# A gated recurrence with a feed-forward block: the first block's states aligned and its y formed ahead of a check's result, late gates and three other steps in another order

## The chip, the cores and the metric

The kernel runs on one core of a Trainium2 chip. The metric is device time in microseconds (us) of one execution. Its engines have queues of their own and meet through semaphores only: TensorE (PE, matmul), VectorE (DVE), ScalarE (ACT), GpSimd (POOL), SyncE (SP, which issues DMAs).

## The reference

```python
def layer(x, W_in, b_in, W_gate, b_gate, A, Bm, C, D, W_out, b_out):
    u = x @ W_in + b_in
    g = sigmoid(x @ W_gate + b_gate)
    def step(h_prev, (u_t, g_t, x_t)):
        h_t = tanh(h_prev @ A + u_t @ Bm)
        y_t = h_t @ C.T + u_t @ D.T
        return h_t, g_t * y_t + (1 - g_t) * x_t
    return scan(step) @ W_out + b_out + x
def ffn(x, w1, b1, w2, b2):      # w1, w2 binarized: row mean of |w| times sign(w)
    return gelu(x @ bw1.T + b1) @ bw2.T + b2
x = layernorm(x + layer(x))
x = layernorm(x + ffn(x))
```

x has 2 sequences of 4096 rows of 256, the state 64, the hidden layer 1024 values. All is float32.

## The kernel before

The recurrence is sequential. The kernel cuts each sequence in 64 chunks of 64 steps and runs the 128 chunks side by side, one per column. It first runs the last 40 steps of every chunk from zero to guess the state with which the next one starts, and then all 64 steps from the guess (`sweep1`). `hu` holds for each step the state (partitions 0 to 63) and u (64 to 127); the state that belongs to a step is in the next slot. Steps go in blocks of four (16 blocks, `NB`), each a tile of 128 x 512 for either half of the 256 values.

**The check.** After the last step VectorE compares the end states with the guesses (lines 1246 to 1251: difference, largest, flag per row), TensorE counts the flags (918), VectorE casts the count to an integer (1253), and VectorE, ScalarE and TensorE each load it and branch. If the guesses were off by more than 2^-18 a repair runs the recurrence again 64 times. It isn't needed with these inputs, so all three jump over it. After it VectorE writes two small copies (1262, 1263); the first lets GpSimd go on, which sits still until then.

**The passage.** What follows ties the recurrence to the feed-forward blocks. By step, and with the line that the profile names:

- gates: TensorE multiplies x by W_gate (828 with operands split in a high and a low part, for blocks up to 11; 814 for 12 to 15), ScalarE applies the sigmoid (522). A gate is done in halves, one per 128 outputs, in banks 0 and 1. `GATED` is 11: blocks 11 to 15 are left for the passage.
- `align(n)` (1408): four VectorE copies move the states of block n one slot down, each after the one before, so that state and u of a step stand in one slot. Blocks 0 and 1 only.
- `whole_y_products(n)` (936): y from the aligned slots, in banks 2 and 3. From block 2 on `y_products` (947) takes split operands instead: `hu_high` on ScalarE (580) and `hu_low` on GpSimd (376).
- `less_x`, `gate_y` (VectorE, 1268 and 1274), `mix` (GpSimd, 384): gate times (y - x), plus x. `ys_high` (ScalarE, 560) and `ys_low` (GpSimd, 388) split it.
- `out_products` (TensorE, 965): times W_out, for a pair of row tiles. `add_bias` (GpSimd, 394) adds half of b_out to the reloaded x.
- `first_sum` (VectorE, 1280; it waits for both), spread and moments (1286, 1292), `first_rstd` (GpSimd, 410 and 412), `first_norm` (VectorE, 1302).
- for blocks 0 and 1 `x1_transposes` (TensorE, 974), then `x1_hi` (ScalarE, 569) and `x1_lo` (VectorE, 1314). `residual` (GpSimd, 404) adds b2.
- the feed-forward block in eight chunks c: `hidden` (TensorE, 991), gelu and `hidden_hi` (ScalarE, 585, 593), `hidden_lo` (VectorE, 1319), `ffn_out` (TensorE, 1003). hidden(c) waits for the low part of chunk c - 3.

The order on every engine is written out by hand in the program, and each does its list strictly in that order. From block 1 on `iteration(n)` gives each engine the same list for every block.

Of the kernel before, what the change touches and what calls it, by code (L numbers as in the profile page):

```python
# [39 lines left out]
P = 128  # L40
# [10 lines left out]
def gated_rnn_ffn(nc, x, W_in, b_in, W_gate, b_gate, A, Bm, C, D, W_out, b_out, w1, b1, w2, b2, out):  # L51
# [21 lines left out]
    with ExitStack() as ctx:  # L73
# [3 lines left out]
        def sem(name):  # L77
            return ctx.enter_context(nc.semaphore(name))
# [100 lines left out]
        s_shift = sem("states_aligned")  # L179
        s_huhi = sem("hu_hi_ready")  # L180
# [156 lines left out]
        def _(pool):  # L337
# [48 lines left out]
            def ys_low(b, m):  # L386
                pool.wait_ge(s_yhi, b * KD + m + 1)
                pool.tensor_tensor(ys_lo[:, m, :], gT[:, b, m, :], ys_hi[:, m, :].bitcast(F32),  # L388
                                   ALU.subtract).then_inc(s_ylo, 1)

            def add_bias(b):

                pool.wait_ge(s_xl, b * 16 + 16)
                pool.tensor_tensor(x_load[:, :, :], x_load[:, :, :],  # L394
                                   half_b_out[:, None, :].broadcast_to([P, STEPS, DM]), ALU.add).then_inc(s_xb, 1)
# [11 lines left out]
            def first_rstd(b, pair):  # L407
                tiles = slice(2 * pair, 2 * pair + 2)
                pool.wait_ge(s_v1, b * 2 + pair + 1)
                pool.tensor_tensor(rstd1[:, tiles], moments[:, 0, tiles, 1], eps[:, tiles], ALU.add).then_inc(s_e1, 1)  # L410
                pool.wait_ge(s_e1, b * 2 + pair + 1)
                pool.tensor_tensor(rstd1[:, tiles], rstd1[:, tiles], neg_half[:, tiles], ALU.pow).then_inc(s_rs1, 1)
# [41 lines left out]
            add_bias(0)  # L454
# [3 lines left out]
            ys_low(0, 1)  # L458
            first_rstd(0, 0)
# [41 lines left out]
        def _(act):  # L501
# [18 lines left out]
            def gate(j, m):  # L520
                act.wait_ge(s_gmm, j * KD + m + 1)
                nc.scalar.activation(gT[:, j, m, :], bank[m][:, :], ACT.Sigmoid,
                                     bias=b_gate_col[:, m:m + 1]).then_inc(s_g, 1)
# [129 lines left out]
            gate(GATED, 1)  # L653
            gate(GATED + 1, 0)
            ys_high(0, 0)
            gate(GATED + 1, 1)
            ys_high(0, 1)
# [7 lines left out]
            x1_hi(0, 1)  # L665
            ys_high(1, 1)
            gate(GATED + 3, 1)
            gate(GATED + 4, 0)
            gate(GATED + 4, 1)
# [13 lines left out]
            hidden_gelu(0, 5)  # L683
            x1_hi(1, 0)
            hidden_hi(0, 5)
# [34 lines left out]
        def _(pe):  # L720
# [197 lines left out]
            nc.tensor.matmul(bank[6][0:1, 0:1], gap_flag, ones[0:NS, 0:1], start=True, stop=True).then_inc(s_cnt, 1)  # L918
            gate_half(GATED, 1, gate_parts, 1)
# [11 lines left out]
            def whole_y_products(n):  # L931
                pe.wait_ge(s_shift, n * STEPS + STEPS)
                for m in range(KD):
                    if n > 0:
                        pe.wait_ge(s_t, n * KD - KD + m + 1)
                    nc.tensor.matmul(bank[2 + m][:, :], cd_t[:, m * P:(m + 1) * P],
                                     hu[:, bass.ds(n * STEPS, STEPS), :].rearrange("p s r -> p (s r)"),
                                     start=True, stop=True).then_inc(s_ymm, 1)
# [103 lines left out]
            pe.wait_ge(s_wsplit, 2)  # L1042

            whole_y_products(0)
            gate_half(GATED + 1, 1, gate_product)
            gate_half(GATED + 2, 0, gate_product)
            gate_half(GATED + 2, 1, gate_product)
            for pair in range(2):
                out_products(0, pair)
            whole_y_products(1)  # L1050
            gate_half(GATED + 3, 0, gate_product)
            for pair in range(2):
                x1_transposes(0, pair)
            gate_half(GATED + 3, 1, gate_product)
            gate_half(GATED + 4, 0, gate_product)
            gate_half(GATED + 4, 1, gate_product)
# [3 lines left out]

            hidden(0, 0)
            hidden(0, 1)
            out_products(1, 0)
# [10 lines left out]
            ffn_out(0, 3)  # L1074
            x1_transposes(1, 0)
            hidden(0, 6)
            x1_transposes(1, 1)
            y_products(3, 0)
            hidden(0, 7)
            ffn_out(0, 4)  # L1080
# [25 lines left out]
        def _(dve):  # L1106
# [138 lines left out]

            dve.wait_ge(s_h, 1 + WARM + L)
# [4 lines left out]
            nc.vector.tensor_scalar(gap_flag, gap_max, GUESS_TOLERANCE, None, ALU.is_gt).then_inc(s_cmp, 1)  # L1251
            dve.wait_ge(s_cnt, 1)
# [3 lines left out]
            with dve.If(differ):  # L1256
                nc.vector.tensor_copy(guess, end_state).then_inc(s_rh, 1)
                with dve.Fori(1, CHUNKS) as r:
                    dve.wait_ge(s_rh, r * (L + 1))
                    nc.vector.tensor_copy(guess, end_state).then_inc(s_rh, 1)  # L1260
                dve.wait_ge(s_rh, CHUNKS * (L + 1))
            nc.vector.tensor_copy(small[:, 31:32], inv_scale).then_inc(s_done, 1)
# [140 lines left out]
            def align(n):  # L1403

                for step in range(n * STEPS, (n + 1) * STEPS):
                    if step > 0:
                        dve.wait_ge(s_shift, step)
                    nc.vector.tensor_copy(hu[0:NS, step, :], hu[0:NS, step + 1, :]).then_inc(s_shift, 1)


            align(0)
# [37 lines left out]
            hidden_lo(0, 4)  # L1449
            x1_lo(1, 0)  # L1450
            hidden_lo(0, 5)
# [70 lines left out]
```

## Time and profile before

Median of 3 runs 459.25 us (457.73 to 459.54). The profiled execution took 457.62 us, its span (first to last instruction) is 455.8 us at a mean granted TensorE clock of 0.989.

| engine | busy us | share of the span | instructions |
|---|---|---|---|
| TensorE, matmul | 430.1 | 94% | 2719 |
| TensorE, weight load | 307.0 | 67% | 2719 |
| VectorE | 372.6 | 82% | 800 |
| ScalarE | 313.0 | 69% | 578 |
| GpSimd | 271.0 | 59% | 289 |

The recurrence ends near 119.7 us, the last gate is done near 148.9 us, and the rhythm of the feed-forward blocks begins near 172 us. The end of a matmul is modelled, so that the next may start a little ahead of it. In a timeline's row the idle time of the engine ahead of the row and the instruction that ended it stand in brackets.

### The profile page before, as it was taken

The page shows a single profiled execution, that of the slowest core. Times are in us where ns is not written, and L with a number is a line of the kernel's source. Part 1 is how long each engine was busy: PE and PEld are TensorE (multiplying, and loading weights), DVE is VectorE, ACT ScalarE, POOL GpSimd, SP SyncE. Part 2 cuts the span into 40 slices and gives each one's busy share as a digit, 9 for nine tenths or more (in the row PEclk, how much of TensorE's full clock was granted, in tenths as well). Part 3 has the DMA queues.
Part 4 walks back from the last instruction along what each step waited for, and adds up shares of the span by engine and source line. Part 5 has one row for each costly group of instructions (what it writes and reads, how often), then busy time and mean ns, then how long its engine had stood idle before and what let it go on. Part 6 is the DMA issues. An engine that isn't in the chain of part 4 may idle for free.

```text
span 455.8 us, 8144 instructions
## 1 busy us (share of the span) xinstructions
PE 430.1 (94%) x2719; PEld 307.0 (67%) x2719; DVE 372.6 (82%) x800; ACT 313.0 (69%) x578; POOL 271.0 (59%) x289
## 2 busy tenths in 40 slices
PE   7999999899988989999999999999999999999981
PEld 4878777587653656767768677677686776766550
DVE  3666678964476669999999999999999999999575
ACT  1222224435533767798988989989889898797792
POOL 5100022523247698879779798798797977673311
PEclk9999999989999999999999999999999999999996
DMA  7544350000101101452534515524245144341413
GB/s 237 175 139 139 103 221 1 1 0 1 46 2 46 41 7 46 55 76 57 93 109 77 95 61 79 127 59 93 95 72 114 47 94 107 80 94 46 47 47 139
DMA packets 38839, 36.13 MB, mean 79 GB/s; under 512 B 31344, under 2 KB 32112, under 8 KB 38672
## 3 DMA queue, kind: packets, MB, share of 16 engines
q1 hardware_dynamic: 37472, 34.61, 30.6%
q0 software_dynamic: 272, 0.66, 0.4%
q10 hardware_dynamic: 1056, 0.36, 0.3%
q8 instruction: 22, 0.36, 0.3%
q14 instruction: 17, 0.14, 0.1%
HBM read 19.90 MB, written 8.39 MB: 62 GB/s over the span
## 4 chain that ended last, share of the span: by engine, by line
PE 60%; DVE 22%; POOL 5%; ACT 5%; issue 5%; DMA 1%; SPq 0%; DVEq 0%; POOLq 0%; ACTq 0%
PE bank L1003 14%; PE bank L991 12%; PE bank L965 9%; DVE hid L1319 7%; PE bank L740 6%; PE bank L733 6%; PE bank L828 5%; ACT hid L593 3%; PE bank L725 3%; DVE gT L1332 3%; DVE bank L1302 3%; PE bank L947 2%; DVE bank L1325 2%; POOL xg_lo L371 2%; DVE gT L1314 2%
## 5 line engine op out<-in xcount | busy, mean ns | idle before, releaser
L991 PE MATMUL bank<-xT,w1s 128*128 128x512 f16 x512 | 126.9, 380 | 2.9 <-DVE hid L1319 2.2
L1003 PE MATMUL bank<-w2s,hid 128*128 128x256 f16 x1024 | 125.5, 273 | 1.0 <-DVE gT L1332 0.8
L1003 PEld LDWEIGHTS bank<-w2s,hid 128*128 128x128 f16 x1024 | 98.6, 98 | 31.7 <-issue 5.6
L585 ACT ACTIVATE bank<-bank,b_col,alpha 128x512 f32<-128x512 f32 x128 | 96.8, 756 | 17.2 <-PE bank L991 17.1
L1319 DVE SCALAR_TENSOR_TENSOR hid<-bank,small,hid 128x512 f16<-128x512 f32 x128 | 94.4, 739 | 14.6 <-ACT hid L593 14.6
L593 ACT ACTIVATE hid<-bank,small 128x512 f16<-128x512 f32 x128 | 86.5, 691 | 18.6 <-PE bank L1003 17.4
L991 PEld LDWEIGHTS bank<-xT,w1s 128*128 128x128 f16 x512 | 46.0, 98 | 49.8 <-DVE hid L1319 7.4
L371 POOL TENSOR_TENSOR xg_lo<-xT,xg_hi 128x512 fp32r<-128x512 f32 x12 | 19.1, 1615 | 80.2 <-DVE xg_hi L1135 80.2
L388 POOL TENSOR_TENSOR ys_lo<-gT,ys_hi 128x512 fp32r<-128x512 f32 x32 | 40.8, 1278 | 24.5 <-ACT ys_hi L560 24.4
L384 POOL TENSOR_TENSOR gT<-gT,xT 128x512 f32<-128x512 f32 x32 | 40.8, 1276 | 18.6 <-DVE gT L1274 18.4
L740 PE MATMUL bank<-hu,w_rec 128*128 128x128 f32 x208 | 46.8, 307 | 1.9 <-DVE hu L1114 0.9
L529 ACT ACTIVATE hu<-bank 64x128 f32 (+1 forms) x64 | 17.4, 272 | 40.5 <-PE bank L740 38.7
L740 PEld LDWEIGHTS bank<-hu,w_rec 128*128 128x128 f32 x208 | 32.0, 190 | 18.3 <-ACT hu L529 7.7
L404 POOL TENSOR_TENSOR gT<-x_rows,b_row 128x1024 f32<-128x1024 f32 x16 | 38.0, 2378 | 9.6 <-DMA xT<-gT 9.5
L394 POOL TENSOR_TENSOR x_load<-x_load,half_b_out 128x1024 f32<-128x1024 f32 x16 | 37.8, 2364 | 8.1 <-DMA x_load<-in_L_attn_x 8.1
L965 PE MATMUL bank<-w_out_hi,ys_hi 128*128 128x256 f32 x128 | 39.1, 305 | 0.6 <-POOL ys_lo L388 0.6
L733 PE MATMUL bank<-xT,w_in 128*128 128x256 f32 x128 | 37.9, 380 | 0.0
L376 POOL TENSOR_TENSOR hu_lo<-hu,hu_hi 64x512 fp32r<-64x512 f32 x28 | 35.4, 1265 | 2.2
L965 PE MATMUL bank<-w_out_hi,ys_lo 128*128 128x256 f32 x128 | 36.0, 281 | 0.0
L965 PE MATMUL bank<-w_out_lo,ys_hi 128*128 128x256 f32 x128 | 36.0, 281 | 0.0
L599 ACT ACTIVATE gT<-gT,shift,rstd 128x256 f32<-128x256 f32 x60 | 34.7, 616 | 0.0
L1109 DVE COPY xT<-bank 128x256 f32 (+1 forms) x64 | 25.4, 422 | 9.5 <-PE bank L725 8.5
(136 smaller groups left out, 777.0 us busy)
## 6 DMA issues: line engine op xcount, KB each, us to landing
x_load<-in_L_attn_x SPq DMA_DIRECT2D x16, 512.0 KB, 3.3
gT<-in_L_attn_x SPq DMA_DIRECT2D x15, 512.0 KB, 3.4
out_rows<-gT SPq DMA_DIRECT2D x15, 512.0 KB, 2.6
gT<-in_L_ffn_w SPq DMA_DIRECT2D x2, 1024.0 KB, 7.7
gT<-in_L_attn_x SPq DMA_DIRECT2D x4, 128.0 KB, 2.7
out_rows<-gT SPq DMA_DIRECT2D x2, 256.0 KB, 2.2
xT<-gT SPq DMA_TRANSPOSE x28, 4.1
w_gate<-in_L_attn_W_gate ACTq DMA_DIRECT2D x1, 256.0 KB, 7.4
```

Source lines behind the costliest of these rows:

```text
L384: pool.tensor_tensor(gT[:, b, m, :], gT[:, b, m, :], xT[:, b, m, :], ALU.add).then_inc(s_ys, 1)
L388: pool.tensor_tensor(ys_lo[:, m, :], gT[:, b, m, :], ys_hi[:, m, :].bitcast(F32), ALU.subtract).then_inc(s_ylo, 1)
L394: pool.tensor_tensor(x_load[:, :, :], x_load[:, :, :], half_b_out[:, None, :].broadcast_to([P, STEPS, DM]), ALU.add).then_inc(s_xb, 1)
L404: pool.tensor_tensor(rows_of(gT, b), x1_rows[:, :, :], b2_row[:, None, :].broadcast_to([P, STEPS, DM]), ALU.add).then_inc(s_x1b, 1)
L585: nc.scalar.activation(bank[which][:, :], bank[which][:, :], ACT.Gelu, bias=b1_col[:, c:c + 1], scale=alpha1[:, c:c + 1]).then_inc(s_gelu, 1)
L593: nc.scalar.activation(hid[:, c % 3, 0, :], bank[HIDDEN_BANKS[c % 3]][:, :], ACT.Copy, scale=hid_scale[:, 0:1]).then_inc(s_hhi, 1)
L733: done = nc.tensor.matmul(bank[4 + half][:, 0:N // 2], w_in[:, k, :], xT[:, j, k, half * (N // 2):(half + 1) * (N // 2)], start=(k == 0), ...
L740: nc.tensor.matmul(bank[6 + parity][:, 0:P], w_rec[:, :], hu[:, t, :], start=True, stop=True).then_inc(done_sem, 1)
L965: done = nc.tensor.matmul(bank[6 + pair][:, e * DM:(e + 1) * DM], ys, w[:, k, :], start=(i == 0), stop=(i == len(parts) - 1))
L991: done = nc.tensor.matmul(bank[which][:, :], w1s[:, k, c * P:(c + 1) * P], x1T[:, n, :, part, :, k, :], start=(k == 0 and part == 0), stop ...
L1003: done = nc.tensor.matmul(bank[tile // 2][:, tile % 2 * DM:(tile % 2 + 1) * DM], hid[:, c % 3, part, tile * P:(tile + 1) * P], w2s[:, c, : ...
L1319: nc.vector.scalar_tensor_tensor(out=hid[:, c % 3, 1, :], in0=bank[HIDDEN_BANKS[c % 3]][:, :], scalar=hid_scale[:, 0:1], in1=hid[:, c % 3, ...
```

## The change

The four copies of `align(0)` stand on VectorE right behind the flag's computation, ahead of the flag copy and the branch. `whole_y_products(0)` stands on TensorE behind the count's product, ahead of the second half of gate block 11. In the branch that isn't taken, the repair first waits for this y, clears slot 0, runs, aligns the states again and forms y again. On GpSimd the bias addition of block 0 goes behind that block's mixes and low parts. TensorE's gates of blocks 13 and later are placed otherwise among the output and transposing steps, and ScalarE's list follows; `hidden(0, 7)` goes ahead of the second transposes of block 1 and `y_products(3, 0)` behind `ffn_out(0, 4)`.

```diff
 # GpSimd
-            add_bias(0)
             mix(0, 0)
             mix(0, 1)
             ys_low(0, 0)
             ys_low(0, 1)
+            add_bias(0)
             first_rstd(0, 0)
 # ScalarE
             gate(GATED, 1)
+            ys_high(0, 0)
             gate(GATED + 1, 0)
-            ys_high(0, 0)
+            ys_high(0, 1)
             gate(GATED + 1, 1)
-            ys_high(0, 1)
             gate(GATED + 2, 0)
...
             gate(GATED + 3, 0)
             x1_hi(0, 0)
             ys_high(1, 0)
-            x1_hi(0, 1)
-            ys_high(1, 1)
             gate(GATED + 3, 1)
             gate(GATED + 4, 0)
+            ys_high(1, 1)
+            x1_hi(0, 1)
             gate(GATED + 4, 1)
...
             hidden_gelu(0, 5)
+            hidden_hi(0, 5)
             x1_hi(1, 0)
-            hidden_hi(0, 5)
             x1_hi(1, 1)
 # TensorE
             nc.tensor.matmul(bank[6][0:1, 0:1], gap_flag, ones[0:NS, 0:1], start=True, stop=True).then_inc(s_cnt, 1)
+            def whole_y_products(n):
+                pe.wait_ge(s_shift, n * STEPS + STEPS)
+                for m in range(KD):
+                    if n > 0:
+                        pe.wait_ge(s_t, n * KD - KD + m + 1)
+                    nc.tensor.matmul(bank[2 + m][:, :], cd_t[:, m * P:(m + 1) * P],
+                                     hu[:, bass.ds(n * STEPS, STEPS), :].rearrange("p s r -> p (s r)"),
+                                     start=True, stop=True).then_inc(s_ymm, 1)
+            whole_y_products(0)
             gate_half(GATED, 1, gate_parts, 1)
             gate_half(GATED + 1, 0, gate_product)
             pe.wait_ge(s_flag, 1)
...
-            pe.wait_ge(s_wsplit, 2)
-            whole_y_products(0)
             gate_half(GATED + 1, 1, gate_product)
             gate_half(GATED + 2, 0, gate_product)
-            gate_half(GATED + 2, 1, gate_product)
+            pe.wait_ge(s_wsplit, 2)
             for pair in range(2):
                 out_products(0, pair)
             whole_y_products(1)
+            gate_half(GATED + 2, 1, gate_product)
             gate_half(GATED + 3, 0, gate_product)
-            for pair in range(2):
-                x1_transposes(0, pair)
+            x1_transposes(0, 0)
             gate_half(GATED + 3, 1, gate_product)
             gate_half(GATED + 4, 0, gate_product)
+            x1_transposes(0, 1)
             gate_half(GATED + 4, 1, gate_product)
...
+            out_products(1, 0)
             hidden(0, 0)
             hidden(0, 1)
-            out_products(1, 0)
             y_products(2, 0)
...
+            hidden(0, 6)
             x1_transposes(1, 0)
-            hidden(0, 6)
+            hidden(0, 7)
             x1_transposes(1, 1)
+            ffn_out(0, 4)
             y_products(3, 0)
-            hidden(0, 7)
-            ffn_out(0, 4)
             out_products(2, 0)
 # VectorE
             nc.vector.tensor_scalar(gap_flag, gap_max, GUESS_TOLERANCE, None, ALU.is_gt).then_inc(s_cmp, 1)
+            align(0)
             dve.wait_ge(s_cnt, 1)
             nc.vector.tensor_copy(flag_i[:, :], bank[6][0:1, 0:1]).then_inc(s_flag, 1)
             dve.wait_ge(s_flag, 1)
             differ = dve.value_load(flag_i[0:1, 0:1], min_val=0, max_val=NS)
             with dve.If(differ):
+                dve.wait_ge(s_ymm, KD)
+                nc.vector.memset(hu[0:NS, 0, :], 0.0).then_inc(s_redo, 1)
+                dve.wait_ge(s_redo, 1)
                 nc.vector.tensor_copy(guess, end_state).then_inc(s_rh, 1)
...
                 dve.wait_ge(s_rh, CHUNKS * (L + 1))
+                for step in range(STEPS):
+                    dve.wait_ge(s_redo, step + 1)
+                    nc.vector.tensor_copy(hu[0:NS, step, :], hu[0:NS, step + 1, :]).then_inc(s_redo, 1)
+                dve.wait_ge(s_yagain, KD)
...
-            align(0)
             less_x(0, 0)
...
             hidden_lo(0, 4)
+            hidden_lo(0, 5)
             x1_lo(1, 0)
-            hidden_lo(0, 5)
             x1_lo(1, 1)
```

TensorE's part of the repair likewise waits for the states aligned again and forms y again.

## Rows read from the trace of the kernel before

**Rows 1.** Waits of TensorE, 121 to 173 us: waiter, cause: total us, times, longest

```profile
PE bank L974 <- DVE x_rows L1302: 3.0, 3, 1.1
PE bank L936 <- DVE hu L1408: 1.4, 1, 1.4
...
PE bank L965 <- POOL ys_lo L388: 0.6, 1, 0.6
```

**Rows 2.** The chain of waits, two aligning copies of block 0: start us, us, what

```profile
123.12 0.23 DVE hu L1408
...
123.62 2.35 DVE hu L1408
```

**Rows 3.** Timeline of VectorE, check to blocks: start us, us, engine, line, operation

```profile
120.33 0.15 DVE L1251 TENSOR_SCALAR small<-small 64x1 f32<-64x1 f32 x1
121.42 0.15 DVE L1253 CAST flag_i<-bank 1x1 int32<-1x1 f32 x1 [0.94 <-PE bank L918]
122.74 0.15 DVE L1262 COPY small<-small 128x1 f32<-128x1 f32 x1 [1.18 <-issue]
...
127.25 0.70 DVE L1268 TENSOR_TENSOR bank<-bank,xT 128x512 f32<-128x512 f32 x1 [1.28 <-PE bank L936]
...
129.92 3.96 DVE L1408 COPY hu<-hu 64x128 f32<-64x128 f32 x4
135.60 0.70 DVE L1280 SCALAR_TENSOR_TENSOR bank<-x_load,bank 128x512 f32<-128x512 f32 x1 [1.72 <-PE bank L965]
...
140.51 0.98 DVE L1302 TENSOR_SCALAR x_rows<-bank,moments,rstd 128x256 f32<-128x256 f32 x2
...
152.92 0.70 DVE L1268 TENSOR_TENSOR bank<-bank,xT 128x512 f32<-128x512 f32 x1
...
164.39 0.74 DVE L1319 SCALAR_TENSOR_TENSOR hid<-bank,small,hid 128x512 f16<-128x512 f32 x1
...
170.26 0.70 DVE L1280 SCALAR_TENSOR_TENSOR bank<-x_load,bank 128x512 f32<-128x512 f32 x1 [1.76 <-PE bank L965]
...
174.31 1.00 DVE L1302 TENSOR_SCALAR bank<-bank,moments,rstd 128x256 f32<-128x256 f32 x2
...
176.63 0.71 DVE L1319 SCALAR_TENSOR_TENSOR hid<-bank,small,hid 128x512 f16<-128x512 f32 x1
...
195.02 0.75 DVE L1319 SCALAR_TENSOR_TENSOR hid<-bank,small,hid 128x512 f16<-128x512 f32 x1 [0.40 <-ACT hid L593]
```

**Rows 4.** Timeline of GpSimd, the passage

```profile
123.55 2.34 POOL L394 TENSOR_TENSOR x_load<-x_load,half_b_out 128x1024 f32<-128x1024 f32 x1 [8.11 <-DMA x_load<-in_L_attn_x]
128.75 2.60 POOL L384 TENSOR_TENSOR gT<-gT,xT 128x512 f32<-128x512 f32 x2 [2.86 <-DVE gT L1274]
...
145.11 1.27 POOL L388 TENSOR_TENSOR ys_lo<-gT,ys_hi 128x512 fp32r<-128x512 f32 x1 [0.41 <-ACT ys_hi L560]
...
148.76 2.62 POOL L376 TENSOR_TENSOR hu_lo<-hu,hu_hi 64x512 fp32r<-64x512 f32 x2
...
169.67 1.28 POOL L384 TENSOR_TENSOR gT<-gT,xT 128x512 f32<-128x512 f32 x1
170.92 2.38 POOL L404 TENSOR_TENSOR gT<-x_rows,b_row 128x1024 f32<-128x1024 f32 x1
```

**Rows 5.** Timeline of TensorE: three gate halves, output product of block 0, y of block 1

```profile
127.90 5.39 PE L814 MATMUL bank<-xT,w_gate 128*128 128x512 f32 x12
133.86 0.39 PE L965 MATMUL bank<-w_out_hi,ys_hi 128*128 128x256 f32 x1 [0.56 <-POOL ys_lo L388]
...
136.84 1.88 PE L936 MATMUL bank<-hu,hid 128*128 128x512 f32 x4
```

**Rows 6.** Timeline of ScalarE: one high part of ys

```profile
144.41 0.62 ACT L560 ACTIVATE ys_hi<-gT 128x512 fp32r<-128x512 f32 x1
```

**Rows 7.** A stretch by itself: bounds, us, busy us of each engine (instructions), clock, DMA

```profile
90.00:94.00 4.00, 4.00 (x16) 3.23 (x14) 3.43 (x11) 1.70 (x5) 0.29 (x1) 0.57 0.00 0
```

**Rows 8.** Waits of TensorE, 40 to 121 us, columns as in group 1

```profile
PE bank L828 <- POOL xg_lo L371: 2.0, 1, 2.0
```

More of the change, by code:

```diff
@@ L179, in gated_rnn_ffn @@
         s_shift = sem("states_aligned")
+        s_yagain = sem("y_product_after_repair")
+        s_redo = sem("states_aligned_after_repair")
         s_huhi = sem("hu_hi_ready")
@@ L929, in _ @@
                             scan_step(j * 2 + s, s, s_rscan)
-            def whole_y_products(n):
-                pe.wait_ge(s_shift, n * STEPS + STEPS)
+                pe.wait_ge(s_redo, STEPS + 1)
                 for m in range(KD):
-                    if n > 0:
-                        pe.wait_ge(s_t, n * KD - KD + m + 1)
                     nc.tensor.matmul(bank[2 + m][:, :], cd_t[:, m * P:(m + 1) * P],
-                                     hu[:, bass.ds(n * STEPS, STEPS), :].rearrange("p s r -> p (s r)"),
-                                     start=True, stop=True).then_inc(s_ymm, 1)
+                                     hu[:, 0:STEPS, :].rearrange("p s r -> p (s r)"),
+                                     start=True, stop=True).then_inc(s_yagain, 1)
             def y_products(n, m):
@@ L1244, in _, with align @@
                     gate_x_lo(n)
+            def align(n):
+                for step in range(n * STEPS, (n + 1) * STEPS):
+                    if step > 0:
+                        dve.wait_ge(s_shift, step)
+                    nc.vector.tensor_copy(hu[0:NS, step, :], hu[0:NS, step + 1, :]).then_inc(s_shift, 1)
             dve.wait_ge(s_h, 1 + WARM + L)
@@ L1401, in iteration @@
                     hidden_lo(n, 5)
[L1403 to L1408, printed above, removed]
-            align(0)
             less_x(0, 0)
```

## The prediction

> **What bounds the kernel now.** I read the views in this order: the page's first part, the waits of TensorE, the timelines of the engines over the passage between recurrence and feed-forward blocks, the chain of waits, and last two stretches that set bounds. The first part has TensorE busy for 94% of the span, so only its idle time can be won. The waits show where that lies in the passage [rows 1]: 1.4 us for the first aligned states, 0.6 us for the low part of the first ys, and 3.0 us in three waits for normalised rows: 1.1 and 1.0 ahead of the two transposes of block 0 and 0.9 ahead of the second of block 1. After the passage the same instruction, the low part of hidden chunk 0, starts at 176.63 and 195.02 [rows 3], 18.39 us apart and so in the blocks' common rhythm; what is won by 176.63 should last to the end, and nothing behind it changes.
>
> The first wait has two causes. VectorE ends the comparison at 120.48, waits for the count, starts the flag copy at 121.42 and the next real instruction at 122.74, 1.32 us later [rows 3]. Only then come the four aligning copies. In the chain of waits one takes 0.23 us, but another 2.35 us [rows 2]: it lasts from 123.62 to 125.97, and GpSimd's bias addition runs from 123.55 to 125.89 [rows 4]. The copies of block 1 take 3.96 us for four [rows 3], beside GpSimd additions of about 1.3 us each. So a copy of this kind stands still while GpSimd works, and costs about 0.25 us when it doesn't.
>
> The Trainium skill says the same in "SBUF — State Buffer", on the port pair that VectorE and GpSimd share: the instruction that comes first holds the pair to its end. It adds that issue order decides who is blocked. By that half of the rule block 1's copies could in the new schedule hold GpSimd up; I come back to it below.
>
> **The change part by part.** All is worked out against the profiled execution (span 455.8, its own time 457.62), which lies 1.63 under the median 459.25.
>
> *Aligning and y of block 0.* The copies now start at 120.5. GpSimd waits for the flag's outcome and is idle, so four cost 4 x 0.25 = 1.0 and end at 121.5. The flag copy follows at once (its count arrives at 121.4 as before) and the branch ends 1.32 later, at 122.8; two small copies, and VectorE can subtract x at 123.0. TensorE starts y at about 121.55: it was to end the count's product at 121.4, so 0.2 us of idle is added, and the three waits queued behind (the other half of gate block 11, the next gate, the flag) come 1.7 us later, which costs nothing: their readers are ScalarE gates that nobody in the passage waits for so early. y's first half is ready 1.28 after the last copy (125.97 to 127.25 [rows 2, 3]), at 122.8. So the subtraction moves from 127.25 to 123.0, 4.25 earlier. If GpSimd did block the copies, the cost would be as before, 3.1, and the gain 2.1 less.
>
> *GpSimd's order.* The two mixes start 1.50 after the subtraction (127.25 to 128.75) and take 2.60 [rows 3, 4]: 124.5 to 127.1. Two low parts at 1.27 each follow at once, since the bias addition now stands behind them: 129.6. ScalarE's high parts are ready (0.62 each [rows 6], the first at 126.4, the second behind the gate at 127.4 to 128.0). The bias addition then runs from 129.6 to 131.95 (2.34).
> TensorE meanwhile: y 1.72, the gate half with parts 1.5, then three gate halves. Twelve gate records in 5.39 with their tail [rows 5], 1.72 a half, so it reaches the output product at 129.95, 0.35 after its input. That product was at 133.86. Its two pairs take 2.98 (133.86 to 136.84 [rows 5]).
> The first sum needs the product's first pair (start + 1.74, from 133.86 to 135.60 [rows 3, 5]: 131.7) and now also the bias, at 132.0. So 132.0 for 135.60: 3.6 earlier. The move of the bias addition costs 0.3 here and saves 2.34 of GpSimd in front.
>
> *Gates dealt out anew.* VectorE is dense from the first sum to the first norm (135.60 to 140.51 and 0.98 for it [rows 3]): its rows are ready 5.9 after the sum, at 137.9. TensorE: outputs to 132.9, y(1) to 134.65, two gate halves to 138.1, and the transposes start without a wait. Two gates, the other transposes (0.5), one gate: the last ends at 144.3. The waits of 1.4, 0.6 and twice about 1.05 are gone, 4.1 us by the view of waits; the same stretches are 4.8 us long from the regular end of the one row to the start of the next, and that is what moves the last gate's end from 148.87 to 144.3.
>
> *What is late next.* The high part of ys of block 1, half 1 now stands on ScalarE behind the gate of 15, half 0. TensorE ends that gate at 142.0, ScalarE's gate runs to 142.9, the high part to 143.45. GpSimd's low part was at 145.11 [rows 4], now it is at 143.5: only 1.6 of the 4.5 are left. GpSimd's order from there is fixed: 1.23 for this, 2.4 for the bias, then two low parts of the states (148.76 to 151.38 before, a start 3.65 after 145.11), so they end at 149.8. TensorE waits 0.5 us for the output product of block 1 (144.8) and then 1.8 us for y(2,0), at 149.85. The subtraction on VectorE was at 152.92, right behind the first sum and so not waiting; it now waits for its product, 1.0 behind: 150.8. From here VectorE and GpSimd are dense in turn as before, 2.1 early.
> The low part of chunk 4 moves from 164.39 [rows 3] to 162.3. TensorE now takes hidden(7) before the second transposes and y(3,0) after ffn(4), and so waits for that low part until 163.1; hidden 0.87, transposes 0.5, ffn 0.87, y(3,0) at 165.4, output product at 166.1. The first sum of block 2 is then at 167.8 for 170.26: 2.45 early, since one wait replaces two. But y(3,0) itself was at 166.07 and gains only 0.7. Its gated result reaches GpSimd's mix at 167.85 (169.67 before), then the residual 1.25 later, and the norm of block 2 starts 4.64 behind the mix, as before (169.67 to 174.31 [rows 3, 4]): 172.5. VectorE was dense from 170.26 to 174.31 and would be there at 171.85, so 0.65 of the 2.45 goes. From that norm on VectorE sets the pace to hidden(4) of block 1, 1.8 us early.
>
> **Sum:** 4.25 won at the start, 0.65 back to the bias and the product's order (3.6 left), 1.5 back in GpSimd's order (2.1), 0.35 won at TensorE's last wait, 0.65 back at GpSimd's mix: **-1.8 us**. 457.62 - 1.8 = 455.8 for a profiled execution, 459.25 - 1.8 = **457.4** for the median. The repair's additions are skipped; they cost only if the longer jump does. The jump as it is lies within the 1.32 us; twice that at VectorE would be +1.3 at the start, bounds 0 and 1.3, and I take 0, as the jump is one instruction either way.
>
> By the skill's rule on issue order the four copies of block 1 (from 125.65) could each hold GpSimd for 0.25: up to 1.0 us on the way to the output product, of which 0.35 is covered, so the result by it would be near -1.2. The rows speak against it: the two mixes that ran into such copies took 2.60 together [rows 4]. I leave it out of the sum.
>
> **The rivals.**
> A, y(3,0) doesn't matter: if VectorE gets other work in the 0.65, or ScalarE's next blocks take up the slack, 2.45 passes: 456.8. For it: VectorE's rhythm has 0.40 of idle in each block, ahead of 195.02 [rows 3]. Against: that idle lies behind the norm, not ahead of it.
> B, most of the gain goes: GpSimd has one place more in which it is late, by one of its pieces of 1.27, or the jump costs 1.3. Then -0.5: 458.7. For it: GpSimd's low parts decide twice, with TensorE's work only 0.35 and 0.15 away in two other places. Against: every order after 143.5 is that of before.
> C, slower: TensorE's clock. Of the waits before, one of 2.0 us on the path to 89.05 [rows 8] was followed by a stretch 90 to 94 at 0.57 of full clock [rows 7], that is, at its lower level of 1.2 GHz for most of it; it loses 4 x 0.43 = 1.7 us. The wait of 1.4 had no such sequel. The new schedule gathers waits of 1.8 us before y(2,0) and 1.7 before hidden(7). If both bring the clock down and TensorE's work there is all on the path, -1.8 + 3.4 = +1.6: 460.9; with one of them -0.1: 459.2. [...]
> The Trainium skill has in "TensorE: Matmul & The Clock Gate", on the clock gate, that idleness brings the array to half rate; the trace agrees with 0.57 after the 2.0 us. It would give the time of C.
> D, the change doesn't do what it says: something holds an early copy as GpSimd's addition does now. Then the start gains 2.1 less, TensorE idles for it, and all behind is shifted: +0.3, 459.6. Against: GpSimd has nothing to do until the check's outcome.
>
> **How the numbers follow.** Forecast 0.53, own range 456.4 to 458.4 (half of each term that goes back, either way). A 0.20, B 0.12, C 0.09 (both stretches 0.03), D 0.06. A median of three runs here moves by 1.8 us, so 0.5% (2.3 us, below 456.95) is what can be told from no change. Of the forecast a fifth falls under 456.95, of A somewhat over half, and some of the rest by the spread of runs: faster 0.32. Slower by 0.5% (over 461.55) needs C twice or a bad spread: 0.05. Same: 0.63. The range is 455.6 to 459.6: it takes in A, B, C with one stretch, and the edge of D.
>
> **What would show it.** Right: L1408's first four copies near 0.25 each, at 120.5; y at 121.6; the output product near 130.0 and its first sum at 132.0; the last gate ending near 144.3; TensorE waiting 1.8 us for GpSimd's low part of the states near 149.8, and about 1.7 for hidden(7); the norm of block 2 waiting for GpSimd near 172.5; the chunk-0 low part of block 1 at 174.8 for 176.63. Wrong: a copy over 1 us in the first four, a granted clock under 1.0 between 144 and 173, a first sum of block 2 and norm that are 2.4 early both (A), or a rhythm other than 18.4 us after the passage.

## The result and the profile after

The changed kernel takes 454.81 us (median of 20 runs, 453.33 to 456.39), the kernel before 457.87 in the same comparison (20 runs, the three shown ahead of the prediction among them, 454.11 to 461.0): ratio 0.9935, 95% interval 0.9916 to 0.9955, that is 3.0 us less (2.1 to 3.8). The forecast was 457.4 with a range down to 455.6, so it was too high, and its range missed. In a later comparison (e12) the same kernel gave 0.9973 (0.9954 to 0.9993; 454.14 for 455.62).

The profiled execution took 456.39 us, span 454.6. It reached the comparison later than before's, at 121.44 for 120.33. Each of the two had a stretch at about half clock ahead of it, this one at 11 to 15 us and before's at 90 to 94 [rows 7]; a second profile of the changed kernel (e12), which had none, is there at 118.56. So in what follows times are counted **from the start of the instruction that ends the comparison** (120.33 before, 121.44 after). VectorE's timeline, the rows that answer to [rows 3]:

```profile
121.44 0.15 DVE L1266 TENSOR_SCALAR small<-small 64x1 f32<-64x1 f32 x1
121.51 0.97 DVE L1259 COPY hu<-hu 64x128 f32<-64x128 f32 x4
...
123.94 0.69 DVE L1292 TENSOR_TENSOR bank<-bank,xT 128x512 f32<-128x512 f32 x1
...
126.60 3.96 DVE L1259 COPY hu<-hu 64x128 f32<-64x128 f32 x4
132.93 0.70 DVE L1304 SCALAR_TENSOR_TENSOR bank<-x_load,bank 128x512 f32<-128x512 f32 x1 [2.37 <-POOL x_load L396]
...
151.57 0.70 DVE L1292 TENSOR_TENSOR bank<-bank,xT 128x512 f32<-128x512 f32 x1 [2.93 <-PE bank L957]
...
163.03 1.40 DVE L1343 SCALAR_TENSOR_TENSOR hid<-bank,small,hid 128x512 f16<-128x512 f32 x2
...
168.47 0.70 DVE L1304 SCALAR_TENSOR_TENSOR bank<-x_load,bank 128x512 f32<-128x512 f32 x1
...
173.01 1.00 DVE L1326 TENSOR_SCALAR bank<-bank,moments,rstd 128x256 f32<-128x256 f32 x2 [0.40 <-POOL rstd L414]
...
175.34 0.72 DVE L1343 SCALAR_TENSOR_TENSOR hid<-bank,small,hid 128x512 f16<-128x512 f32 x1
...
193.72 0.75 DVE L1343 SCALAR_TENSOR_TENSOR hid<-bank,small,hid 128x512 f16<-128x512 f32 x1 [0.40 <-ACT hid L595]
```

The reader is to see three things. The four copies take 0.97 us. The first sum waits for the bias addition, not for the product. The norm of block 2 waits 0.40 us for GpSimd, and the rhythm behind it is 18.38 us (175.34 to 193.72), as before. TensorE's waits, 119 to 173 us:

```profile
PE bank L1001 <- DVE hid L1343: 1.8, 1, 1.8
PE bank L957 <- POOL hu_lo L378: 1.4, 1, 1.4
PE bank L975 <- POOL ys_lo L390: 0.7, 1, 0.7
...
```

and the granted clock over the same stretch (columns as in [rows 7]):

```profile
119.00:173.00 54.00, 49.84 (x254) 32.17 (x254) 35.24 (x76) 30.86 (x49) 37.49 (x32) 1.00 0.10 30
```

TensorE's timeline, to compare with [rows 5]: the gates end without a gap before the output product, which starts 9.2 us behind the comparison for 13.5, and the last gate begins at 21.8.

```profile
125.73 5.31 PE L816 MATMUL bank<-xT,w_gate 128*128 128x512 f32 x12
130.62 0.54 PE L975 MATMUL bank<-w_out_hi,ys_hi 128*128 128x256 f32 x1
...
143.21 1.88 PE L816 MATMUL bank<-xT,w_gate 128*128 128x512 f32 x4
```

And GpSimd's timeline, where the gain was given back (compare [rows 4]):

```profile
144.26 1.26 POOL L390 TENSOR_TENSOR ys_lo<-gT,ys_hi 128x512 fp32r<-128x512 f32 x1 [2.12 <-ACT ys_hi L562]
145.48 2.36 POOL L396 TENSOR_TENSOR x_load<-x_load,half_b_out 128x1024 f32<-128x1024 f32 x1
147.92 2.60 POOL L378 TENSOR_TENSOR hu_lo<-hu,hu_hi 64x512 fp32r<-64x512 f32 x2
```

In this table (VectorE's starts, counted as said; "end" is the last instruction of the span) are all kernels; e1 to e12 are the experiments below. "Loss" marks a stretch at about half clock inside the passage; "a copy held" means that one of the four copies stood still while GpSimd worked.

| kernel | first subtraction | first sum, block 0 | subtraction, block 2 | low part, chunk 4 | first sum, block 2 | chunk 0, block 1 | end | |
|---|---|---|---|---|---|---|---|---|
| before, first profile | 6.92 | 15.27 | 32.59 | 44.06 | 49.93 | 56.30 | 335.47 | a copy held |
| before, second (e8) | 5.21 | 13.57 | 32.58 | 44.05 | 49.92 | 56.29 | 335.57 | copies free, loss at 141 |
| changed | 2.50 | 11.49 | 30.13 | 41.59 | 47.03 | 53.90 | 333.16 | |
| changed again (e12) | 2.54 | 11.54 | 30.19 | 41.66 | 47.09 | 53.97 | 333.24 | |
| e1 | 2.54 | 12.81 | 30.14 | 41.61 | 49.13 | 55.50 | 334.72 | loss at 164 |
| e2 | 5.22 | 14.23 | 32.88 | 44.34 | 49.77 | 56.63 | 335.88 | |
| e3 | 2.53 | 11.52 | 28.46 | 39.93 | 45.36 | 52.23 | 331.49 | |
| e4 | 2.52 | 11.52 | 30.15 | 41.63 | 49.14 | 55.52 | 334.74 | loss at 165 |
| e5 | 5.21 | 14.24 | 31.52 | 42.98 | 48.84 | 55.21 | 334.57 | |
| e6 | 5.21 | 13.73 | 31.06 | 42.53 | 48.40 | 54.77 | 334.13 | |
| e7 | 6.89 | 15.23 | 32.55 | 44.01 | 49.45 | 56.31 | 335.66 | a copy held |
| e9 | 2.53 | 11.54 | 28.48 | 37.56 | 45.41 | 52.16 | 331.49 | |
| e10 | 2.55 | 11.55 | 28.49 | 38.04 | 44.55 | 51.30 | 330.51 | |
| e11 | 5.23 | 13.58 | 30.89 | 42.36 | 49.87 | 56.24 | 335.52 | loss at 162 |

So by the two profiles 2.3 us are gained at the end (335.47 - 333.16), where 1.8 were forecast. Before with free copies and no loss has no profile of its own; by the second profile less its loss it would end at 333.9 (335.57 - 1.65, an estimate; how the 1.65 is found stands under e1), 0.7 behind the changed kernel.

### The profile page after: what moved, and what is told of

The parts are those of the page before. It is cut to its first block, busy times and chain, and to the rows that moved or that the text cites. A ratio compares the mean times of both kernels' runs of the same rounds, so it can differ in the third digit from the quotient of the medians.

```text
span 454.6 us, 8144 instructions
## 1 busy us (share of the span) xinstructions
PE 429.4 (94%) x2719; PEld 307.1 (68%) x2719; DVE 370.6 (82%) x800; ACT 313.0 (69%) x578; POOL 270.6 (60%) x289
## 4 chain that ended last, share of the span: by engine, by line
PE 61%; DVE 19%; POOL 6%; ACT 6%; issue 5%; DMA 2%; SPq 0%; POOLq 0%; DVEq 0%; ACTq 0%
PE bank L1013 14%; PE bank L1001 11%; PE bank L975 9%; DVE hid L1343 7%; PE bank L742 7%; PE bank L735 6%; PE bank L830 6%; ACT hid L595 3%; PE bank L727 3%; DVE gT L1356 3%; DVE bank L1326 3%; PE bank L957 2%; DVE bank L1349 2%; PE bank L816 2%; DVE gT L1338 2%
## 5 line engine op out<-in xcount | busy, mean ns | idle before, releaser
L519 ACT ACTIVATE hu<-bank 64x128 f32 x40 | 10.9, 272 | 34.6 <-PE bank L742 34.6
```

## The experiments

The first four undo or isolate parts of the change; e5 to e8 ask what the time of before is made of; the last four test the remedy and what sets the end of the passage. A ratio is to the kernel before, in the same comparison on one chip: e1 to e4 on one, e5 to e8 on a second, the rest on a third.

**e1_early_y.** Before, with the early alignment and y alone.

```diff
+            align(0)                      # VectorE, ahead of the flag copy
+            whole_y_products(0)           # TensorE, ahead of gate block 11, half 1
```

> Before, with one part of the change alone: states of block 0 aligned and y formed ahead of the count's result; every order (bias addition, late gates, tail of the passage) as before. Theory 1 (the early start carries the gain; the late gates only decide what is given back): bias addition of block 0 runs about 123.5 to 125.9 before the mixes, so the first sum of block 0 comes 2.1 us earlier than before (133.5 for 135.6, measured from the same end of the recurrence), GpSimd's chain follows 2.1 earlier, and by the low part of hidden chunk 0 of block 1 about -2.1 us is left, nearly as much as the whole change shows (-2.4 in its trace). Theory 2 (the gates dealt out anew carry it, by hiding TensorE's waits for norms): these waits stay, under -0.8. Theory 3 (before, some executions lose TensorE's clock in the passage): then the spread of times shrinks with the 1.4 us wait gone.

Ratio 1.0012 (0.9986 to 1.0037): no gain over before can be told, which by itself would fit theory 2. In its profile the step works as theory 1 says up to the low part of chunk 4: 41.61, the changed kernel's 41.59, and 2.45 less than before. The whole gain of the passage up to there comes from this part. But then 1.65 us are lost: from that low part to chunk 0 of block 1 it takes 13.89 us, before 12.24. The granted clock (last but two of the columns: bounds, length, busy us of five engines, clock, DMA share, GB/s) says why:

```profile
119.00:164.00 45.00, 41.06 (x191) 24.75 (x189) 28.84 (x63) 26.17 (x43) 29.43 (x26) 1.00 0.13 36
164.00:168.00 4.00, 3.93 (x13) 2.00 (x14) 2.38 (x4) 1.86 (x3) 3.92 (x4) 0.57 0.00 0
```

Ahead of it TensorE waits 0.9 us, makes four transposes, and waits 0.9 us again; the same two waits stand in before's first profile, without a loss. So 0.8 is left at chunk 0 (55.50 for 56.30) of the 2.1 expected there.

The mean clock of an execution tells how many such stretches it had: in the fourteen profiles it is 0.992 to 0.994 with none ahead of the last 15 us, 0.988 to 0.990 with one, wherever it lay, and 0.984 or 0.985 with two. None of e1's 12 executions has 0.992 or more, eight have under 0.988; of before's 31 in that comparison ten and seven.

**e2_order_only.** The changed kernel without the early start.

```diff
-            whole_y_products(0)           # back behind the branch
-            align(0)                      # back behind the two small copies
```

> The changed kernel with block 0 aligned and its y formed after the check's outcome again, as before; bias addition, late gates, ScalarE's list and the tail in the new order. Theory 1: y starts as before, the bias addition now delays the first sum by 0.6 us, ScalarE's high part of ys (block 1, half 1) waits for the gate of block 15, half 0 and comes 2.4 us later than before, and y(2,0) 1.8 later; the tail gives 0.3 back: slower than before by about 1.2 to 1.8 us. Theory 2: TensorE's waits for norms are hidden, so faster than before by 1.5 to 2 us.

Ratio 1.0033 (1.0004 to 1.0062), 457.81 us: slower, as theory 1 said, and theory 2 has fallen. In the trace it ends 0.4 later than before's first profile, although its copies are free (0.97), and 0.3 later than before's second, although it has no loss in the passage; that is 2.0 behind the estimate for before with neither (333.9), where 1.2 to 1.8 more than before were expected. Without the early start the new order costs time.

**e3_high_part_first.**

```diff
             gate(GATED + 3, 1)
+            ys_high(1, 1)
             gate(GATED + 4, 0)
-            ys_high(1, 1)
```

> The changed kernel with ScalarE taking the high part of ys (block 1, half 1) ahead of the gate of block 15, half 0 instead of behind it. Theory 1: what was given back was lost here, in GpSimd's chain: its low part starts near 142.2 instead of 144.3, the states' low parts end 2 us earlier, TensorE's wait of 1.4 us ahead of y(2,0) goes, and 1.4 us (1.0 to 2.0) beyond the change is won. Rival: TensorE's own work sets y(2,0) or VectorE the rest, under 0.4 us.

Ratio 0.9916 (0.9888 to 0.9944), 451.91 us. The end comes 1.67 earlier than in the changed kernel. Its wait for the states' low part falls from 1.4 to 0.6 us, and GpSimd's low part of ys (block 1, half 1) is

```profile
139.23 1.27 POOL L390 TENSOR_TENSOR ys_lo<-gT,ys_hi 128x512 fp32r<-128x512 f32 x1 [0.40 <-ACT ys_hi L562]
```

This is 21.1 us behind the comparison (118.11) for 22.8 in the changed kernel (144.26 less 121.44): the place of the give-back was right.

**e4_tail_as_before.**

```diff
-            hidden(0, 6)
             x1_transposes(1, 0)
-            hidden(0, 7)
+            hidden(0, 6)
             x1_transposes(1, 1)
-            ffn_out(0, 4)
             y_products(3, 0)
+            hidden(0, 7)
+            ffn_out(0, 4)
```

> The changed kernel with TensorE's tail of the passage as before: transposes(1,0), hidden(6), transposes(1,1), y(3,0), hidden(7), ffn(4). Theory 1 (as I forecast the step): the first sum of block 2 comes 0.35 later than in the changed kernel but y(3,0) and GpSimd's mix come earlier, VectorE's norm of block 2 no longer waits 0.4 for GpSimd; net within 0.3 us of the changed kernel. Rival A of the prediction (y(3,0)'s place doesn't matter): 0.35 to 0.5 us slower than the changed kernel.

455.55 us, ratio 0.9995 (0.9974 to 1.0016): no gain over before can be told. The changed kernel wasn't timed in this comparison, but e3, which is 1.67 us ahead of it in the trace, stands at 451.91 here, 3.6 under e4. Neither expected size was right. Its profile too has a loss, as e1's:

```profile
165.00:169.00 4.00, 4.00 (x19) 2.70 (x18) 1.36 (x2) 1.51 (x3) 4.00 (x4) 0.57 0.00 0
```

Without those 1.65 us chunk 0 of block 1 would be at 53.87, against 53.90: in an execution without a loss the tail's order is worth nothing, as forecast within 0.3. What it is worth lies in the clocks: of e4's 12 executions none has 0.992 or more and four have under 0.988, of the 32 of the changed kernel (20 and e12's 12, in other comparisons) 14 and none.

**e5_bias_behind.**

```diff
-            add_bias(0)
             mix(0, 0)
...
             ys_low(0, 1)
+            add_bias(0)
```

> Before, with one part of the change alone: GpSimd's bias addition of block 0 behind that block's mixes and low parts. Theory 1 (the copy of 2.35 us was held by this addition): block 0's four copies fall from 3.1 to 1.0 us, y starts behind gate block 12, half 0 (1.6 earlier), and the first sum, which now waits for the bias, is 1.0 earlier; about -1.0 us against an execution of before in which a copy was held. Theory 4 (before has two modes: held, as in its profile, and free, when the reloaded x lands after the copies): this kernel is always free, so its own times at equal granted clock lie in one group, and its gain over the mean of before is under 1 us. Rival (the copy is slow by itself): no change in the copies and +0.6 us.

Ratio 1.0003 (0.9971 to 1.0035); in the trace 0.9 less than before's first profile, copies 0.97. Its twelve times at equal clock do not lie in one group (454.17 to 455.26 at 0.992 and above), so that part of the expectation isn't borne out. The first sum waits for the bias at 14.24, and the end is 0.7 behind the 333.9 estimated for before with free copies: the move by itself frees the copies and costs some of it back.

**e6_load_later.**

```diff
-            sp.wait_ge(s_gmm, GATED * KD)
+            sp.wait_ge(s_gmm, GATED * KD + 1)
```

> Before, with SyncE's reload of x for block 0 released one gate half later (after half 0 of block 11, about 1.4 us), nothing else changed. Theory 1 and 4: the bias addition then starts after the copies, they take 1.0 us, and the kernel is about 1.5 us faster than before's profiled, held mode (y 1.6 earlier, the first sum 1.5), with one group of times at equal clock; if before is often free already, the gain over its mean is 0.5 to 1.0. Rival: the addition, later by 1.4, delays the mixes more than the copies gain: no gain or slower.

Ratio 1.0009 (0.9982 to 1.0037). Only the time of a transfer differs, and the copies are free: GpSimd's addition starts at 124.96, the copies run from 122.77 to 123.74, and the trace ends 1.3 earlier than before's first profile. So it was the addition that held the copy of 2.35 us, as read in the prediction. The median doesn't follow, and the gain of 0.5 to 1.0 over before's mean isn't there. That would be so if before were seldom held in these comparisons, and its times fit: of the 21 executions of before with a mean clock of 0.992 or more on the three chips 19 take 453.54 to 454.66 us and two 455.13 and 455.93, where a held copy should add 1.6.

**e7_tail_new.**

```diff
+            hidden(0, 6)
             x1_transposes(1, 0)
-            hidden(0, 6)
+            hidden(0, 7)
             x1_transposes(1, 1)
+            ffn_out(0, 4)
             y_products(3, 0)
-            hidden(0, 7)
-            ffn_out(0, 4)
```

> Before, with TensorE's new tail of the passage alone: hidden(6), transposes(1,0), hidden(7), transposes(1,1), ffn(4), y(3,0). Theory 3 (with the old tail TensorE's clock falls to half in some executions, as 165 to 168 us in the profiles of e1 and e4; the new tail prevents it): no stretch under full clock between 119 and 175, mean clock of an execution never as low as in before's worst, and times 0.3 to 1.2 us under before on average, 0.2 to 0.4 where no clock is lost. Rival (the clock fell by chance of the start, the tail has no part in it): the same distribution of clocks as before, and within 0.3 us.

Ratio 0.9999 (0.9976 to 1.0021), copies held at 3.08. The tail step alone: the first sum of block 2 comes 0.48 earlier than before (49.45), the norm waits 0.40 for GpSimd, and at chunk 0 nothing is left (56.31 for 56.30). One of 12 executions has a mean clock under 0.988, of before in that comparison 6 of 35, too few to tell apart. The 0.3 to 1.2 us of theory 3 are not borne out: by itself the new tail shows no gain.

**e8_before_again.** The kernel before, no edit.

> The kernel before itself, profiled anew. Theory 4 (two modes): either the third or another copy of block 0 again takes over 2 us, or all four take 1.0 together and the rest from the check's end to the last instruction is about 1.8 us shorter than in the first profile (335.5 us). If theory 3 holds as well, a stretch at half clock may stand between 164 and 169. Rival: it is as in the first profile, and the spread of before has its causes ahead of the passage alone.

This is the telling one: the same span as the first profile, 455.8 us, by other means, which none of the expected outcomes had. VectorE's copies and GpSimd's addition:

```profile
122.73 0.97 DVE L1408 COPY hu<-hu 64x128 f32<-64x128 f32 x4
```

```profile
123.57 2.35 POOL L394 TENSOR_TENSOR x_load<-x_load,half_b_out 128x1024 f32<-128x1024 f32 x1 [8.25 <-DMA x_load<-in_L_attn_x]
```

All four copies have been started when the addition starts (122.73 plus three times 0.25 is 123.48). In the first profile the last one was due at 123.62 [rows 2] and the addition started at 123.55 [rows 4]: 0.1 us decide over 2.1. The first sum came 1.7 earlier in this execution, and this took it away again:

```profile
119.00:141.00 22.00, 19.72 (x74) 10.98 (x72) 15.37 (x36) 8.68 (x16) 11.03 (x11) 1.00 0.17 49
141.00:144.50 3.50, 3.08 (x7) 1.85 (x8) 1.66 (x3) 1.67 (x4) 2.69 (x3) 0.58 0.00 0
```

TensorE's lower level, 1.2 GHz, for most of 3.5 us, after it had waited 1.1 us, made four transposes and waited 1.0 us. The first profile has the same two waits and transposes at full clock, and so have those of e1, e6 and e7.

The 12 executions have a median of 456.87, ratio 1.0015 (0.9980 to 1.0049) to the other 35 of the same kernel: medians of twelve that lie 1 us apart say little here.

**e11_waits_filled.**

```diff
             for pair in range(2):
+                nc.tensor.matmul(bank[5][:, :], w_gate[:, 0, 0:P], xT[:, NB - 1, 0, :], start=True, stop=True)
                 x1_transposes(0, pair)
```

The products' results are used nowhere.

> Before, with one product that nothing needs (128 x 512 in float32, 0.86 us, into a bank that is free) ahead of each of the two transposing steps of block 0, in TensorE's waits of 1.1 and 1.0 us. It adds 1.7 us of work and removes nothing. Theory 3 (in some executions TensorE's clock falls after these waits, 141 to 144.5 in the second profile of before, at 1.7 us): the products fit in the waits, no stretch at half clock stands between 119 and 160 in any profile, and its median is 0.2 to 0.8 us under before's, by as often as the clock fell there. Rival (the fall has nothing to do with these waits): 0 to 0.3 us slower and the same spread of clocks.

Ratio 0.9992 (0.9973 to 1.0011), the median 0.2 above before's: the gain of 0.2 to 0.8 isn't borne out, and with one execution of 12 under 0.988 for before's 2 of 23 the clocks don't decide. The subtraction of block 2 comes at 30.89, the 1.7 us of work fit in the waits and the clock is full there, but it falls in the tail:

```profile
162.00:166.00 4.00, 3.98 (x14) 2.02 (x15) 2.32 (x4) 1.85 (x3) 3.96 (x3) 0.57 0.00 0
```

Less its loss it gives the same estimate as e8 for before with free copies and no loss: 56.24 - 1.65 = 54.6 at chunk 0, 333.9 at the end.

**e12_changed_again.** The changed kernel, no edit.

> The changed kernel itself, on the chip of the variants. Theories 3 and 4: its copies are never held and its clock is full from 119 to 175, so its passage from the check's end to the last instruction is 333.2 us as in its first profile, where before has 333.8 at best (free copies, full clock) and 335.5 with either a held copy or a fall of the clock. So 0.3 to 0.6 us over before's best executions at equal clock and 1.5 to 3 us in the medians. Rival (the whole 2.4 us is work moved off the path): 2.4 us also against before's best executions.

Passage to end 333.24, copies 0.97, clock full from 116 to 172 us. Its six executions without a lost stretch (mean clock 0.993 or 0.994) take 453.01 to 453.58; before's four (0.992) on that chip 453.98, 454.04, 454.12 and 455.13. So about 1.0 us by the medians of these and 0.7 by the traces (333.9 - 333.2), more than the 0.3 to 0.6 expected, and 1.5 over all executions: the rival of 2.4 has fallen. The rest of the 1.5 fits the lost stretches. Before has none, one and two of them in 4, 17 and 2 of its executions, the changed kernel in 6, 6 and none, 0.4 fewer on average; at 1.65 us or more each that is 0.7.

**e9_low_part_first.** On top of e3:

```diff
             first_norm(1, 0)
+            hidden_lo(0, 4)
             first_norm(1, 1)
-            hidden_lo(0, 4)
```

> The kernel of e3 (ScalarE's high part ahead of the gate) with VectorE taking the low part of hidden chunk 4 ahead of the second norm of block 1, in the 1.4 us for which it waits for GpSimd there. TensorE's wait of 1.8 us ahead of hidden(7) goes. If TensorE sets the pace there: 1 us or more under e3. If GpSimd does (its chain from the mix of 157 to the norm of 173 is dense in the chain of waits of the changed kernel): y(3,0) then waits for the states' low part, and under 0.4 us is won.

The low part comes 2.4 earlier (37.56 for 39.93), TensorE's wait falls from 1.8 to 0.9, and the end does not move: 331.49 in both. So TensorE doesn't set the pace; whether GpSimd does, e10 asks. Ratio 0.9938 (0.9916 to 0.9959).

**e10_states_low_on_vector.** On top of e9:

```diff
             hidden_lo(0, 3)
+            dve.wait_ge(s_huhi, 3)
+            nc.vector.tensor_tensor(hu_lo[HALVES[0], :, :], beside(3, 0), hu_hi[HALVES[0], :, :].bitcast(F32),
+                                    ALU.subtract).then_inc(s_hulo, 1)
             first_norm(1, 0)
-            hu_low(3, 0)                  # GpSimd
```

> e9 with one of GpSimd's low parts of the states (block 3, half 0; 1.27 us there) done by VectorE (about 0.7 us) ahead of the first norm of block 1, where VectorE waits 0.7 us for GpSimd. If GpSimd's chain sets the end of the passage, as e9 is to show: 0.7 to 1.3 us under e9, and together with e3 the fastest version, 3 us or more under the changed kernel. Rival (VectorE's own work then sets it): within 0.3 us of e9.

451.72 us, ratio 0.9916 (0.9895 to 0.9937), the fastest version. It ends 1.0 before e9 in the trace, as expected, so GpSimd's work was what the end waited for. It is 2.4 us under the changed kernel on the same chip (454.14), where I had expected 3 or more.

## Why the prediction was wrong

**The steps held.** Counted from the comparison, each came in the order given and within 0.7 us:

| step | forecast | measured |
|---|---|---|
| four early copies | 1.0 us | 0.97 |
| first subtraction | 2.7 | 2.50 |
| first sum of block 0 | 11.7, bound by the bias | 11.49, bound by the bias |
| subtraction of block 2 | 30.5 | 30.13 |
| low part of chunk 4 | 42.0 | 41.59 |
| first sum of block 2 | 47.5 | 47.03 |
| norm of block 2 | 52.2, waiting for GpSimd | 51.57, waiting 0.40 |
| chunk 0 of block 1 | 54.5 | 53.90 |

Rival A (y(3,0)'s place doesn't matter) fell: the norm waits, in e2 and e7 as well. B and D fell with the copies at 0.97 and the ends of GpSimd's rows. C, a loss of clock in the passage of the new kernel, showed in neither of its two profiles, in spite of a wait of 1.8 us. The row that C stood on was one execution's: the wait of 2.0 us ahead of 90 us stands in all fourteen profiles, and seven of them have no low stretch behind it, the changed kernel's two among these.

**The sum was 0.5 us short**: "-1.8 us" measured -2.3 between the two profiles, by small shares of each term.

| term | forecast | measured |
|---|---|---|
| won at the start | 4.25 | 4.42 |
| back to the bias and the product's order | 0.65 | 0.64 |
| back in GpSimd's order | 1.5 | 1.32 |
| won at TensorE's last wait | 0.35 | 0.44 |
| back at GpSimd's mix | 0.65 | 0.50 |
| back from chunk 0 to the end | 0 | 0.09 |

The third was too large because TensorE's dense work ended ahead of my count, so that ScalarE's high part of ys, which waits behind the gate of block 15, half 0, starts 22.1 us behind the comparison (143.56) and not 22.5.

**The step that failed is the base.** "All is worked out against the profiled execution (span 455.8, its own time 457.62), which lies 1.63 under the median 459.25" treats before as one schedule, and the median of three runs, 459.25, as its time. Both were wrong. Twenty runs have a median of 457.87: that the three lay 1.4 above it is chance, and the larger half of the miss. ("A median of three runs here moves by 1.8 us" took the spread of the three, 457.73 to 459.54, for what they can do; the twenty spread over 454.11 to 461.0.) And before has several schedules. Its copies are held (+1.6 at the end) or free, by 0.1 us; and in two places of the passage the clock falls in some executions (+1.65 each): at 141 us in its own second profile, and in the tail in the profiles of e1, e4 and e11, which have its order there. In the changed kernel the alignment lies where GpSimd has nothing to do, the waits for block 0's norms are gone, and hidden(6), hidden(7) and ffn(4) stand between what were waits and transposes. Rival C named a loss of clock and put it on the wrong side: I wrote "The wait of 1.4 had no such sequel" and did not ask what two waits of 1 us around four transposes do in the executions that I hadn't seen.

What bears it out beyond the profiles is the mean clock of each execution, which one lost stretch lowers by about 0.004. Under 0.988, so with two or more, lie 38 of the 161 executions of kernels with the old tail (before in three comparisons, e1, e4, e5, e6, e8, e11), 1 of 76 of those with the new one (changed, e2, e3, e7, e9, e10, e12), and none of the 64 among these that also have the new order of gates. These kernels differ in more than the tail, and the mean doesn't say where a stretch lay. The pair that differs in the tail alone is e4 and the changed kernel, 4 of 12 for none of 32; put into the kernel before by itself (e7) the tail shows no such effect, nor does filling the first waits (e11). Which part of the change keeps the clock up in kernels like before is therefore not shown.

**The miss in numbers.** 457.4 - 454.81 = 2.6. Of it 1.4 is the median of before (459.25 for the three runs shown, 457.87 for twenty), 0.5 the sum, and 0.7 what the changed kernel saves in the medians beyond the profiled pair (3.1 for 2.3). That the last is due to before's losses of clock is not shown for that comparison itself, since before's clocks weren't recorded in it. Nor is it settled why the gain was 3.0 us there and 1.2 to 1.5 in e12's comparison; on which chip the first was made isn't recorded. The difference is before's: its median is 457.87 there and 455.62 to 455.85 in the three later comparisons, the changed kernel's 454.81 and 454.14. Copies held in most executions there (+1.6) would fit; no run tells.

Copies that came ahead of GpSimd's addition took 0.25 us each, the one that came 0.07 us behind its start 2.35. The Trainium skill has it so in "SBUF — State Buffer", section "Who interferes with whom": of VectorE and GpSimd, whichever issues first gets the shared port pair for the whole instruction. The half of that rule that I held against the forecast, copies of block 1 holding GpSimd up, did not show: its mixes took 2.50. Rival C had beside it the Trainium skill's "TensorE: Matmul & The Clock Gate", on the clock gate, by which idleness brings the array to half rate; the traces agree with 0.58 behind two waits of about 1 us in e8, and show that the same waits can stay without it, as in before's first profile.

## What to carry to other kernels

Before pricing a change against a trace, ask whether the trace is the only mode: look for a releaser and a rival user of a shared port, or two waits around light work, that lie within a few tenths of a us, and give each mode its time and share. A change can pay by removing a mode as well as by shortening a path (here about half of the 1.5 us of e12), and then its gain is in the mean and not in the best execution. Take the time of before from many runs, since a median of three was 1.4 us off, and sort executions by granted clock before comparing small steps; and where work is dealt out anew between waits, follow the engine that is behind (GpSimd here): moving one ScalarE instruction ahead of one gate won 1.7 us in the trace, shortening TensorE's wait by 0.9 us none.

## What the runs showed of the hardware

Lost stretches of clock lay at 11 to 15, 88 to 94, 141 to 144.5 or 162 to 169 us, in different executions of kernels with the same orders there. In the passage each cost 1.65 to 1.7 us. One at 88 to 94 cost more: the comparison starts at 120.22 to 120.78 behind it, and at 117.83 to 118.89 in the profiles that have none by then.

Waits of 1.4, 0.7 and 1.8 us between products went without one (changed kernel, clock 1.00 throughout 119 to 173). Ahead of each loss in the passage stood two short waits with four transposes between, 1.1 and 1.0 us or 0.9 and 0.9; but so they did in profiles that kept full clock, as in before's first. That they bring it on is a reading, which e11 did not settle.

A copy on VectorE and an addition on GpSimd did not share: whichever began first ran its own time, and 0.1 us decided between four copies in 0.97 and in 3.09 us.
